# Attention prologue and pair steps: each pair's queries and keys are prepared in two halves of the tokens

## What is computed

```python
xn = _rmsnorm(x, gamma1)
q = (xn @ q_w + q_b).reshape(b, s, H, HD).transpose(0, 2, 1, 3)
k = (xn @ k_w + k_b).reshape(b, s, H, HD).transpose(0, 2, 1, 3)
v = (xn @ v_w + v_b).reshape(b, s, H, HD).transpose(0, 2, 1, 3)
q = _rope(q, theta)
k = _rope(k, theta)
scores = jnp.einsum('bhqd,bhkd->bhqk', q, k) * scale
scores = jnp.where(causal, scores, -jnp.inf)
attn = jax.nn.softmax(scores, axis=-1)
ctx = jnp.einsum('bhqk,bhkd->bhqd', attn, v)
attn_out = ctx.transpose(0, 2, 1, 3).reshape(b, s, H * HD) @ o_w + o_b + xn
```

## Time and profile before

| | us |
|---|---|
| median of 3 runs | 2493.31 |
| lowest, highest | 2492.89, 2502.37 |
| the profiled execution, its time | 2495.71 |
| the profiled execution, its span (first to last instruction) | 2493.8 |
| PE busy in the span | 1981.7 (79%) |
| DVE, ACT, POOL busy | 1655.0, 1438.5, 855.7 |

### The profile page before, as it was taken

How to read it: one execution, slowest core, us unless ns; L and a number is a source line. 1 busy time by engine, 2 the same in 40 slices (tenths; PEclk the granted TensorE clock), 3 DMA queues, 4 the chain that set the end, 5 groups by cost and what they waited for, 6 DMA issues and landing times.

```text
span 2493.8 us, 41045 instructions
## 1 busy us (share of the span) xinstructions
PE 1981.7 (79%) x9942; PEld 1292.0 (52%) x9942; DVE 1655.0 (66%) x2947; ACT 1438.5 (58%) x2785; POOL 855.7 (34%) x797
## 2 busy tenths in 40 slices
PE   3738999879773999987966499996996659999698
PEld 1226666547323666655732366664662246666466
DVE  4946676669485666657948566665794756666488
ACT  3516676647452767655744367674674336766366
POOL 1534233133163433403315434331332453343132
PEclk9869999979796999998979699998896979999899
DMA  2011111001001110101100111100100011110011
GB/s 60 0 32 39 31 27 36 1 28 40 10 0 40 31 39 20 35 1 32 36 10 0 51 25 33 32 23 9 31 28 10 12 39 33 26 38 17 10 36 32
DMA packets 65391, 64.33 MB, mean 26 GB/s; under 512 B 12184, under 2 KB 48384, under 8 KB 65280
## 3 DMA queue, kind: packets, MB, share of 16 engines
q1 hardware_dynamic: 65280, 63.01, 9.6%
HBM read 27.31 MB, written 2.10 MB: 12 GB/s over the span
## 4 chain that ended last, share of the span: by engine, by line
PE 52%; DVE 18%; ACT 12%; issue 11%; POOL 3%; ACTq 1%; SPq 1%; DMA 1%; DVEq 1%; POOLq 0%
PE ps L1380 9%; PE ps L1219 6%; PE ps L1221 6%; PE ps L1220 6%; DVE state L959 6%; PE ps L1369 5%; PE ps L1359 4%; ACT probs L724 4%; PE ps L1360 3%; PE ps L1344 2%; PE ps L1486 2%; PE ps L1395 2%; ACT probsT L736 2%; ACT k_high L717 2%; PE ps L1247 2%
## 5 line engine op out<-in xcount | busy, mean ns | idle before, releaser
L736 ACT ACTIVATE probsT<-ps 128x512 f32<-128x512 f32 (+3 forms) x768 | 349.3, 492 | 361.8 <-PE ps L1369 361.8
L1359 PE MATMUL ps<-k_high,q_split 128*128 128x512 f32 (+3 forms) x768 | 312.3, 407 | 133.4 <-DVE q_split L1027 68.3
L724 ACT ACTIVATE probs<-ps,least 128x640 f32<-128x640 f32 (+7 forms) x512 | 380.3, 743 | 53.5 <-DVE least L1037 46.6
L1369 PE MATMUL ps<-ident,probs 128*128 128x128 f32 x2304 | 350.4, 279 | 10.3 <-ACT probsT L736 10.1
L1369 PEld LDWEIGHTS ps<-ident,probs 128*128 128x128 f32 x2304 | 261.8, 141 | 130.6 <-issue 93.0
L1380 PE MATMUL ps<-probsT,vals 128*64 128x512 f32 (+3 forms) x1536 | 292.6, 505 | 21.1 <-ACT probsT L736 21.1
L1044 DVE TENSOR_REDUCE least<-ps 128x1 f32<-128x640 f32 (+3 forms) x256 | 262.2, 1024 | 8.8
L1360 PE MATMUL ps<-k_low,q_split 128*128 128x512 f32 (+3 forms) x768 | 261.2, 352 | 0.0
L1359 PEld LDWEIGHTS ps<-k_high,q_split 128*128 128x128 f32 x768 | 150.1, 195 | 192.2 <-ACT probs L724 110.7
L562 POOL TENSOR_TENSOR roped<-turned,roped 128x512 f32<-128x512 f32 x128 | 163.0, 1274 | 236.8 <-DMA roped<-turned 195.5
L1037 DVE CUSTOM_DVE_ANT_0 ps<-ps,row_masks 128x128 f32<-128x128 f32 (+3 forms) x256 | 127.0, 496 | 166.5 <-PE ps L1360 163.6
(11 more groups left out here) (213 smaller groups left out, 3968.7 us busy)
## 6 DMA issues: line engine op xcount, KB each, us to landing
roped<-turned SPq DMA_DIRECT2D x512, 64.0 KB, 2.0
w<-in_w SPq DMA_DIRECT2D x128, 128.0 KB, 2.0
w_pair<-in_w_pairs SPq DMA_DIRECT2D x36, 128.0 KB, 2.6
xin<-in_x SPq DMA_DIRECT2D x5, 512.0 KB, 3.9
out<-acc SPq DMA_DIRECT2D x4, 512.0 KB, 3.8
pos<-in_c_pos SPq DMA_DIRECT2D x1, 512.0 KB, 4.8
v_w<-in_v_w SPq DMA_DIRECT2D x1, 512.0 KB
o_w<-in_o_w SPq DMA_DIRECT2D x1, 512.0 KB
```

The source lines that it names most:

```text
L724: act.activation(probs[:, t % 2, 0:width(t)], banks(2 * (t % 2))[:, 0:width(t)], ACT.Exp, bias=least[:, t:t + 1], scale=-1.0, accum_out=ro ...
L736: act.activation(dst, ps[:, T_BANK + g % 2, 0:k1 - k0], ACT.Copy).then_inc(t_taken, 1)
L1359: pe.matmul(o, q, k_high[par][h][:, k0:k1], start=True, stop=False)
L1369: made = pe.transpose(ps[:, T_BANK + g % 2, at - k0:at - k0 + P], probs[:, t % 2, at:at + P], ident[:, :])
```

## The change

Each pair's preparation is cut into the first 512 tokens (c = 0) and the second 512 (c = 1).

- The four pieces come in the order keys c = 0, queries c = 0, keys c = 1, queries c = 1.
- Each split instruction takes 512 tokens and there are twice as many: 8 `high` on ACT, 4 copies and 4 `k_low` on POOL, 4 `low` on DVE for a pair. Their slots are new (`HIGH_AT`, `LOW_AT`), and POOL's `widen` (the write of `inverse_wide`) of the same step now stands ahead of the last two `k_low`.
- `scores` waits at unit 0 for the first half and at unit 8 for the second half.
- For a batch's first pair only the first half is prepared ahead of the units. The second half's `high` stand at slots 0 to 3 of its own step, and its `low` at slots 3 and 4. DVE's values come behind the first half's `low`.
- In the prologue `xa` is scaled and turned in halves, ACT writes `xn_high` straight from PSUM and `xnT` behind it, and `xn_low` is made in halves.

The core of the diff (SP's swap loop, the credits and the renamed arguments follow the same split):

```diff
-HIGH_AT = {6: (0, 0), 7: (0, 1), 10: (1, 0), 11: (1, 1)}
-LOW_AT = {12: 0, 13: 1}
+HIGH_AT = {4: (0, 0, 0), 5: (0, 0, 1), 6: (0, 1, 0), 7: (0, 1, 1), 9: (1, 0, 0), 10: (1, 0, 1), 11: (1, 1, 0), 13: (1, 1, 1)}
+FIRST_HIGH_AT = {0: (1, 0, 0), 1: (1, 0, 1), 2: (1, 1, 0), 3: (1, 1, 1)}
+LOW_AT = {7: (0, 0), 8: (0, 1), 12: (1, 0), 14: (1, 1)}
+FIRST_LOW_AT = {3: (1, 0), 4: (1, 1)}
...
                     add(0)
-                    add(1)
-                    pool.wait_ge(roped_ready, 4 * n + 2 + 2)
                     for h in range(2):
                         own, other = slice(HD * h, HD * h + HD), slice(HD - HD * h, P - HD * h)
                         pool.sem_inc(passed, 1)
-                        pool_copy(pool, k_high[par][h][other, :], roped[own, 0, :]).then_inc(high_p, 1)
-                        pool.wait_ge(high_p, 2 * n + h + 1 + 2)
+                        pool_copy(pool, k_high[par][h][other, sl], roped[own, 0, sl]).then_inc(high_p, 1)
+                        pool.wait_ge(high_p, 2 * m + h + 1 + 4)
+                    add(1)
+                    between()
                     for h in range(2):
                         own = slice(HD * h, HD * h + HD)
-                        add(2 + h)
-                        pool.wait_ge(roped_ready, 4 * n + 2 + h + 1 + 2)
-                        pool.sem_inc(passed, 1)
-                        pool.wait_ge(high_a, 4 * n + h + 1 + 4)
-                        pool.tensor_tensor(k_low[par][h][own, :], roped[own, 0, :], k_high[par][h][own, :].bitcast(F32),
+                        pool.wait_ge(high_a, 4 * m + h + 1 + 8)
+                        pool.tensor_tensor(k_low[par][h][own, sl], roped[own, 0, sl], k_high[par][h][own, sl].bitcast(F32),
                                            ALU.subtract).then_inc(low_p, 1)
-                        pool.wait_ge(low_p, 2 * n + h + 1 + 2)
-                    between()
+                        pool.wait_ge(low_p, 2 * m + h + 1 + 4)
...
+                    for c in range(HALVES):
+                        prepare(p + 1, 1 - par, c, lambda k: x_at(p, "proj", k, first, False),
+                                lambda: widen(n, 0, None if first else x_at(p, "old", 0, False, False)) if c else None)
...
                 for c in range(2):
-                    take(14 + c, P, xnT[:, c * HALF:(c + 1) * HALF], ACT.Identity)
-                act.wait_ge(a_taken, b * A_OUTS + 16 + 2)
-                act.activation(xn_high[:, :], xnT[:, :], ACT.Copy).then_inc(xn_high_ready, 1)
...
+                    act.wait_ge(a_out, b * A_OUTS + 14 + c + 1)
+                    act.activation(xn_high[:, cols_of(c)], ps[:, c, :], ACT.Copy)
+                    act.activation(xnT[:, cols_of(c)], ps[:, c, :], ACT.Copy).then_inc(a_taken, 1)
...
+                def high(n, par, c, j, h):
+                    own, sl = slice(HD * h, HD * h + HD), cols_of(c)
+                    act.wait_ge(roped_ready, 2 * (HALVES * n + c) + j + 1 + 2)
+                    act.activation((k_high, q_split)[j][par][h][own, sl], roped[own, j, sl], ACT.Copy,
+                                   scale=(1.0, -SCALE)[j]).then_inc(high_a, 1)
...
+                        if t in FIRST_HIGH_AT and first:
+                            high(n, par, *FIRST_HIGH_AT[t])
                         if t in HIGH_AT and not last:
                             high(n + 1, 1 - par, *HIGH_AT[t])
...
-                for i in range(TILES):
-                    st.did(dve.tensor_scalar(xa[:, i, :], resid[:, i, :], mv[:, i, 0:1], rstd[:, i:i + 1],
-                                             ALU.subtract, ALU.mult))
-                st.wait()
-                made = dve.tensor_tensor(xa[:, :, :], xa[:, :, :], gamma1_r.unsqueeze(1).broadcast_to((P, TILES, P)),
-                                         ALU.mult)
-                made.then_inc(tok_ready, 1)
-
-                dve.wait_ge(xn_high_ready, b + 1)
-                dve.tensor_tensor(xn_low[:, :], xnT[:, :], xn_high[:, :].bitcast(F32), ALU.subtract).then_inc(xn_split, 1)
-
...
+                for c, ready in enumerate((xa_half, tok_ready)):
+                    half = slice(TPH * c, TPH * (c + 1))
+                    for i in range(TPH * c, TPH * (c + 1)):
+                        st.did(dve.tensor_scalar(xa[:, i, :], resid[:, i, :], mv[:, i, 0:1], rstd[:, i:i + 1],
+                                                 ALU.subtract, ALU.mult))
+                    st.wait()
+                    dve.sem_inc(passed, 1)
+                    dve.tensor_tensor(xa[:, half, :], xa[:, half, :], gamma1_r.unsqueeze(1).broadcast_to((P, TPH, P)),
+                                      ALU.mult).then_inc(ready, 1)
+
+                for c in range(2):
+                    sl = cols_of(c)
+                    dve.wait_ge(a_taken, b * A_OUTS + 14 + c + 1 + 2)
+                    dve.tensor_tensor(xn_low[:, sl], xnT[:, sl], xn_high[:, sl].bitcast(F32), ALU.subtract
+                                      ).then_inc(xn_split, 1)
...
-                def low(n, par, h):
-                    own, other = slice(HD * h, HD * h + HD), slice(HD - HD * h, P - HD * h)
-                    dve.wait_ge(high_a, 4 * n + 2 + h + 1 + 4)
-                    dve.scalar_tensor_tensor(q_split[par][h][other, :], roped[own, 1, :], -SCALE,
-                                             q_split[par][h][own, :].bitcast(F32), ALU.mult, ALU.subtract
+                def low(n, par, c, h):
+                    own, other, sl = slice(HD * h, HD * h + HD), slice(HD - HD * h, P - HD * h), cols_of(c)
+                    dve.wait_ge(high_a, 4 * (HALVES * n + c) + 2 + h + 1 + 8)
+                    dve.scalar_tensor_tensor(q_split[par][h][other, sl], roped[own, 1, sl], -SCALE,
+                                             q_split[par][h][own, sl].bitcast(F32), ALU.mult, ALU.subtract
                                              ).then_inc(low_d, 1)
...
+                        if t in FIRST_LOW_AT and first:
+                            low(n, par, *FIRST_LOW_AT[t])
                         if t in LOW_AT and not last:
-                            low(n + 1, 1 - par, LOW_AT[t])
+                            low(n + 1, 1 - par, *LOW_AT[t])
...
+                for h in range(2):
+                    low(b * PAIRS, 0, 0, h)
                 for c in range(2):
                     values(0, 0, 4 + c, c, PROLOGUE_BANK[c])
-                for h in range(2):
-                    low(b * PAIRS, 0, h)
...
-                pe.wait_ge(tok_ready, 3 * b + 2)
-                for c in range(2):
+                for c in range(2):
+                    if c == 0:
+                        pe.wait_ge(xa_half, b + 1)
+                    else:
+                        pe.wait_ge(tok_ready, 3 * b + 2)
...
-                    j, c = divmod(g, 2)
+                    c, j = divmod(g, 2)
...
-                    if t == 0:
-                        pe.wait_ge(high_a, 4 * n + 4 + 4)
-                        pe.wait_ge(high_p, 2 * n + 2 + 2)
-                        pe.wait_ge(low_d, 2 * n + 2 + 2)
-                        pe.wait_ge(low_p, 2 * n + 2 + 2)
+                    if t in (0, TILES):
+                        m = HALVES * n + t // TILES
+                        pe.wait_ge(high_a, 4 * m + 4 + 8)
+                        pe.wait_ge(high_p, 2 * m + 2 + 4)
+                        pe.wait_ge(low_d, 2 * m + 2 + 4)
+                        pe.wait_ge(low_p, 2 * m + 2 + 4)
...
                 for g in range(4):
+                    if g % 2 == 0:
+                        pe.wait_ge(xn_split, 2 * b + g // 2 + 1)
                     project(g, 0, PROLOGUE_BANK[g])
```

80 lines of the change are left out of this document (37 added, 43 removed).

## The result

| | before | after |
|---|---|---|
| median, us (5 runs each) | 2501.92 | 2481.28 |
| lowest, highest | 2492.89, 2502.37 | 2470.65, 2484.55 |
| the profiled execution: time, span | 2495.71, 2493.8 | 2484.55, 2482.4 |

The ratio is 0.9919, with a 95% interval of 0.9901 to 0.9936: about 20 us, or 0.8%, faster. The prediction was 2462 us with a range of 2440 to 2481. So the sign was right, a third of the forecast gain of 32 us did not come, and the time lies just outside the range, near the rival "given back in the steps" (2484). The five runs of before lie in two groups, at 2493 and at 2502 us, and the prediction started from a median of three that lies in the lower group (2493.31).

A forecast was written before the change was run, and what follows sets the result against it. It took attention's serial prologue, about 17 us of idle PE a batch, as the bound. Parts 1 and 2 (-34.8), 3 (+5.2) and 4 (-2.4) gave -32.0 us from 2495.7; with the median 2.4 lower, 2462 us, range 2440 to 2481.

The forecast's parts named there:

- given back in the steps: Rival: first step costs 2.6 us, each middle step 0.6, at places without slack for `high` and `low`; 2484 us, chance 0.16.
- Part 1: Up to the first projection: it starts 0.3 us earlier a batch (bounds 0 and 1.1), with POOL replacing the removed wait.
- Part 2: First sine to first scores: scores at +13.5 us instead of +21.9, a gain of 8.4 us a batch.
- Part 3: First step of a batch, now carrying pair 0's second half: 1.3 us lost (bounds 0 and 3.8), 5.2 for 4 batches.
- Part 4: The 24 middle steps: four places net -0.1 us a step (bounds -0.6 and +0.6), -2.4 us in all.
- a late DVE passes on: +0.3: Middle steps, slots 7 and 8: two DVE `low`, each held up by at most one POOL instruction (1.26 us); PE +0.3.
- The other three places: Middle steps: slot 5 costs PE 0.54 us, slots 6 and 7 leave it 0.2 ahead, slots 12 to 14 gain 0.2.
- The 0.54 of slot 5: Middle steps: a half `k_high` ahead of unit 6's exponential has no slack, so PE loses 0.54 us.
- the 0.74 us behind it: Middle steps, slots 6 and 7: PE's wait for unit 8's exponential takes in the 0.54; PE comes out 0.2 us ahead.
- Slower: Rival: `low` of slots 7 and 8 runs into POOL every middle step, 2.3 us each; 2519 us, chance 0.05.
- More comes out: Rival: engines pass without exclusion and shorter `high` of slots 6 and 7 come through; -53 us, 2442 us, chance 0.17.
- not earlier: Rival: first scores come no earlier, or unit 8's wait takes back unit 0's gain; 2493 us, chance 0.04.

The follow-up runs named there:

- experiment 3: The changed kernel with POOL's `acc` behind the weight splits of pairs 0 and 1 and behind `xn_low`; 2459.20 us, 0.9855 of the kernel before.
- experiment 1: The changed kernel with DVE's four half `low` of a middle step in slots 12 to 15; 2456.38 us, 0.9829 of the kernel before.
- experiment 2: The changed kernel with POOL's second add of each half behind `widen`, DVE's order unchanged; 2456.68 us, 0.9840 of the kernel before.
- Experiment 7: The changed kernel with `low` in slots 12 to 15, `acc` later, first-half `high` in slots 4, 6, 7, 8; 2418.48 us, 0.9690 of before.
- experiments 3 to 5: `acc` moved (0.9855); the changed kernel with all of pair 0 ahead of unit 0 (0.9987); that with unit 0 waiting for both halves (1.0018 of before).
- experiment 8: The changed kernel with `low` in slots 12 to 15, `acc` later, `high` in slots 4, 6, 8 to 13; 2409.74 us, 0.9661 of before.

## Why the prediction was wrong in size

**Part 1** (-0.3 a batch): -0.16, and by the argument given. What takes the place of the removed wait is POOL, and experiment 3 shows that moving POOL's `acc` frees it.

**Part 2** (13.5 us, -8.4): 13.4 us, -8.5. The working by rows and exclusion held to 0.1 us.

**Part 3** (+1.3): +0.6 on average, within 0 and 3.8, but for another reason than mine. I passed the `high` of slot 2 through whole. Unit 5's scores did come 8.0 us behind the first instead of 6.4 to 7.2, but the step made up for most of it. What stayed is the wait of 0.8 us behind the held `low` of slot 7, in three of four batches. With the `low` of slots 7 and 8 moved away (experiment 1) the first step was 40.66 us. Before it was 40.75, and 40.4 in the two batches in which the granted clock did not fall once more in its midst. So the second half in slots 0 to 4 costs 0.3 us at most. PE never waited for it at unit 8, as counted.

**Part 4** (-0.1 a step, bounds -0.6 and +0.6): +0.62, just past the upper bound. This is the step that failed, and two thirds of its error are one term: "a late DVE passes on: +0.3" for slots 7 and 8. I had the mechanism, and its size as up to 1.26 us, and took a quarter, as if the meeting were a matter of chance. But POOL's and DVE's places in a step repeat: in 23 of 24 steps the `low` of slot 8 took 1.53 or 1.54 us, and that cost 0.78 us a step by experiments 1 and 2. I had not put the bound at "every step" either.

The other three places come to -0.17 a step instead of -0.4. The 0.54 of slot 5 was right as a wait (0.56). But the 0.74 us behind it, which was to take this in, fell only to 0.64, so that PE was 0.46 us behind there, not 0.2 ahead. A half `high` takes 0.63 us and not 0.59, which is a small part of it. Experiment 7 shows what leaving slot 5 empty is worth: 1.07 us a step. Elsewhere I had counted too little gain; the wait near 35 us of a step fell from some 0.6 to 0.38, and the rest of that is not traced.

From -32.0 to -19.9 us it is thus +17.2 for the middle steps, -2.9 for the first steps, -2.4 for the last steps and +0.2 for the prologue. The last steps, which prepare nothing, I had left alone. In one of the four the clock stood at its lower level for 3.4 us less, and that one is 1.4 us shorter; the other 1.0 us is not explained. For the prologue and the first step I had counted no change of the clock: in the first step of batch 0 it averages 0.90 before and after.

**Rivals.** "Given back in the steps" came nearest in number, 0.6 us a middle step, but for the wrong reason: not places without slack for `high` and `low` made the steps longer, for with the `low` out of POOL's way they are 0.17 us shorter than before. "Slower" had the right mechanism, but its price of 2.3 us a step (its three terms add up to 2.48) was far too high: PE lost 0.78 to the blocked `low` and not 1.26, and the 0.68 us of load ahead of the smallest of unit 9 does not exist (experiment 2). "More comes out" and "not earlier" did not happen.

## What to carry to other kernels

In a loop whose engines keep their places, a collision between VectorE and GpSimd is no matter of chance: it came in 23 of 24 middle steps, and in 21 or 22 of 24 in experiments 3 to 5, which keep the slots. Price it for every round, at what is left of the other instruction when yours begins (here 0.85 us behind an add of 1.29, of which 0.78 reached PE). Then move one of the two; moving VectorE's `low` or GpSimd's add gave the same 18.9 and 18.8 us. When slots are dealt out, one wait early in a step can be handed around the engines: freeing one slot gave 1.07 us where its own wait was 0.56, and using slot 14 instead of 12 cost 0.7 us in the steps that kept the full clock. The prologue's gain alone would have shown 34 us; two slot tables and the place of `acc` decided whether 20 or 85 us came out (2409.7 us, 0.9661 of before, in experiment 8).
